# The setup of a two-layer transformer kernel made shorter, its modulated rows moved to GpSimd, and the first batch's reciprocals placed behind the next tile's maxima

## The reference, cut to what matters

```python
mod = (_silu(L0_c) @ L0_wmod).reshape(B, 6, 1, -1)         # [16,256] @ [256,1536], once per layer
sa, ca, ga, sb, cb, gb = (mod[:, i] for i in range(6))
ga = (2 * (ga >= 0) - 1) * max(abs(ga), 0.25)              # gb alike
h = layernorm(x) * (1 + ca) + sa
x = x + ga * local_attention_and_mlp(h)                    # q, k, v, band softmax, Wo, layernorm, gelu MLP
h = layernorm(x) * (1 + cb) + sb
x = x + gb * sorted_experts(h)                             # the first 1024 rows, top 2 of 8 experts
# the second layer: mod from L1_c, L1_wmod; linear attention, grouped-query attention, experts by capacity
```

## Time and profile before

| | us |
|---|---|
| median of 3 runs (lowest, highest) | 3178.84 (3176.0, 3182.64) |
| the profiled execution's own time | 3183.52 |
| its span | 3181.8 |
| setup block, until all engines pass its end | 29.1 |
| tile 0 of batch 0: first row maximum | 45.3 |
| tile 0 of batch 1: first row maximum | 94.7 |

### The profile page before, as it was taken

The page is one execution under the profiler, slowest core; times in us unless marked ns, Lnnn a source line. Parts: engine busy times, 40 slices in busy tenths (PEclk is TensorE's granted clock), DMA queues, the critical chain, the costliest instruction groups (busy, mean ns, idle before and its releaser), DMA issues. The chain is left out here.

```text
span 3181.8 us, 58120 instructions
## 1 busy us (share of the span) xinstructions
PE 3018.6 (95%) x19338; PEld 1850.6 (58%) x19338; DVE 2186.8 (69%) x6717; ACT 1562.6 (49%) x3529; POOL 1213.6 (38%) x1530
## 2 busy tenths in 40 slices
PE   7899999999998998899999999999999968999997
PEld 3566766666665674344444444444444327888886
DVE  6777777777763333678888888888888842445545
ACT  3566556565552113466666666666666631111111
POOL 3123232232234212234444444444443242455544
PEclk8899999999999999899999999999999989999998
DMA  8111010110122981222222222222222217999995
GB/s 292 7 53 45 33 64 33 33 64 33 35 100 79 315 297 52 71 58 68 73 74 74 75 71 73 73 77 78 78 78 73 80 35 213 242 272 280 272 263 173
DMA packets 291041, 354.70 MB, mean 111 GB/s; under 512 B 49855, under 2 KB 240562, under 8 KB 290752
## 3 DMA queue, kind: packets, MB, share of 16 engines
q1 hardware_dynamic: 261760, 313.28, 31.2%
q0 software_dynamic: 28464, 34.71, 5.0%
q10 hardware_dynamic: 544, 3.15, 0.3%
HBM read 234.02 MB, written 122.34 MB: 112 GB/s over the span
## 5 line engine op out<-in xcount | busy, mean ns | idle before, releaser
L2907 DVE TENSOR_REDUCE negmax<-psum 128x1 f32<-128x512 f32 x1024 | 670.7, 685 | 129.7 <-PE psum L3487 125.1
L2520 ACT ACTIVATE pT<-psum 128x512 f32<-128x512 f32 x1024 | 576.8, 600 | 258.8 <-PE psum L3513 225.4
L3487 PE MATMUL psum<-k_stack,q_stack 96*128 96x512 bf16 x1024 | 357.0, 388 | 17.4 <-DVE negmax L2907 10.3
L3513 PE MATMUL psum<-q_stack,k_stack 99*128 99x512 bf16 x1024 | 347.8, 382 | 8.1 <-ACT pT L2520 6.2
L4149 POOL DMA_INDIRECT src_rows<-ye,place x142 | 221.9, 1563 | 283.3 <-DVE ye L4208 251.7
L990 ACT ACTIVATE probs<-probs,negmax 128x256 f32<-128x256 f32 x512 | 252.8, 495 | 119.0 <-DVE negmax L1081 117.4
L4166 ACT ACTIVATE actT_x<-psum 128x512 f32<-128x512 f32 x142 | 84.8, 597 | 441.4 <-PE psum L4323 441.4
L3527 PE MATMUL psum<-pT,v_tile 128*32 128x512 f32 x2048 | 273.3, 606 | 1.6 <-ACT pT L2520 1.0
L4323 PE MATMUL psum<-xT_x,w_x 128*128 128x256 f32 x1136 | 260.3, 383 | 1.1 <-DMA w_x<-in_L_ffn_w_dram 1.1
L4335 PE MATMUL psum<-w_x,actT_x 128*128 128x256 f32 x1136 | 256.6, 379 | 0.0
L1081 DVE CUSTOM_DVE_ANT_0 probs<-psum,band_mask 128x256 f32<-128x256 f32 x512 | 181.6, 421 | 104.8 <-PE psum L1339 104.7
(11 more groups left out here) (420 smaller groups left out, 5602.8 us busy)
## 6 DMA issues: line engine op xcount, KB each, us to landing
w_x<-in_L_ffn_w_dram SPq DMA_DIRECT2D x142, 512.0 KB, 5.4
w_e<-in_L_ffn_w_dram SPq DMA_DIRECT2D x46, 1024.0 KB, 6.4
q_stacks<-q_part SPq DMA_DIRECT2D x192, 128.0 KB
q_stack<-q_stacks SPq DMA_DIRECT2D x64, 384.0 KB, 3.7
padded<-w_e SPq DMA_DIRECT2D x32, 650.0 KB, 6.0
xe<-padded SPq DMA_DIRECT2D x71, 260.0 KB, 5.2
gate_rows<-mods SPq DMA_DIRECT2D x66, 256.0 KB, 5.6
src_e<-src_rows SPq DMA_DIRECT2D x30, 512.0 KB, 6.5
```

Source lines behind the costliest of these rows:

```text
L2520: act.activation(pT[:, 4 * (s % 2) + r, :], bank(m, 2 + n % 2), ACT.Exp, scale=float(DHQ) ** -0.5)\
L2907: dve.tensor_reduce(negmax[:, p // REP, h:h + 1], bank(m, max_bank(b, 16 * g + p)), AX.X, ALU.max, negate=True).then_inc(max_read, 1)
L3487: pe.matmul(bank(m, max_bank(b, 16 * g + p)), q_stack[0:K_SCORE, h, t * P:(t + 1) * P], k_stack[0:K_SCORE, g, :], start=True, stop=True).t ...
L3513: pe.matmul(bank(m, 2 + n % 2), k_stack[:, g, kc * P:(kc + 1) * P], q_stack[:, REP * g + r, :], start=True, stop=True).then_inc(sT_done, 1)
```

## The change

Setup computes layer 0's modulation alone, with the columns that batch 0 needs for its projections (two of six slots). Layer 0's nine rows are made in the next block by GpSimd (`first_rows`), ahead of `hidden_rows(0)`. Layer 1's product with `wmod` and the expert counts go into the next block on TensorE. The loads are put in another order, scratch tiles lie in x's room for batches 7 to 15, and VectorE's reciprocals of tiles 0 to 2 in batch 0 stand behind the next tile's maxima. Cut to its core:

```diff
@@ setup_block, SyncE
             for layer in (0, 1):
                 sp.dma_start(cond[:, layer, :], I[f"L{layer}_c"]).then_inc(cond_in, 16)
-            load_batch(0)
...
-            load_attention_weights(sp, m, I)
-            load_batch(1)
+            load_x(sp, m, I, 0, m.x_first)
+            load_attention_weights(sp, m, I)
+            sp.dma_start(m.wmod1[:, :, :], I["L1_wmod"].rearrange("(c p) n -> p c n", p=P)).then_inc(m.x_second, 16)
+            load_x(sp, m, I, 1, m.x_second)
...
             for i, n in enumerate(("L1_attn_bo", "L1_ffn_ob")):
                 sp.dma_start(m.bias1[:, i, :], I[n].partition_broadcast(B)).then_inc(m.bias1_in, 16)
-            sp.wait_ge(rows_ready, 8)
-            sp.dma_start(mods_dram[0, :, :, :], rows[:, :, :]).then_inc(m.rows_out, 16)
+            load_small_weights(sp, m, I)
@@ setup_block, TensorE
+            pe.wait_ge(wmod_in, 16)
+            for n in range(NBLK):
...
             pe.wait_ge(m.xn0_ready, NT)
...
+            pe.wait_ge(scale_ready, 1)
+            for i in (0, 1):
...
@@ local_attention_block, SyncE
+            load_mlp_weights(sp, m, I)
+            sp.wait_ge(rows0_ready, 8)
+            sp.dma_start(mods_dram[0, :, :, :], m.rows0[:, :, :]).then_inc(m.rows_out, 16)
             sp.wait_ge(m.rows_out, 16)
             load_norm_rows(0)
             load_gate_rows(0)
-            load_mlp_weights(sp, m, I)
@@ local_attention_block, GpSimd
+            def first_rows():
+                mod, sign, rows, bias = m.mod0, m.sign0, m.rows0, m.bias0
+                gates = mod[:, 2:6:3, :]
+                step = Steps(pool, rows0_s, 0, 0)
+                step(pool.tensor_scalar(sign[:, :, :], gates, 0.0, 0.5, ALU.is_ge, ALU.subtract))
+                pool.wait_ge(m.bias1_in, 16 * 7)
+                step(pool.tensor_tensor(bias[:, 0, :], bias[:, 0, :], bias[:, 2, :], ALU.add))
+                step.settle()
+                step(pool.tensor_tensor(gates, gates, sign[:, :, :], ALU.mult))
+                pool.tensor_scalar(rows[:, 7, :], mod[:, 4, :], 1.0, None, ALU.add).then_inc(rows0_ready, 1)
+                step.settle()
+                step(pool.tensor_scalar(gates, gates, 0.125, 4.0, ALU.max, ALU.mult))
+                pool.tensor_copy(rows[:, 8, :], mod[:, 3, :]).then_inc(rows0_ready, 1)
+                step.settle()
+                step(pool.tensor_tensor(rows[:, 0:3:2, :], gates, sign[:, :, :], ALU.mult))
+                pool.tensor_copy(rows[:, 4, :], mod[:, 1, :]).then_inc(rows0_ready, 1)
+                step.settle()
...
+                pool.tensor_tensor(rows[:, 1, :], rows[:, 1, :], sign[:, 0, :], ALU.add).then_inc(rows0_ready, 3)
+
+            first_rows()
             hidden_rows(0, 0)
@@ local_attention_block, VectorE, body, for each of tiles 0 to 2
                 if cur:
                     copy_probsT(b, 0)
-                    invert(b, 0)
+                    if not first:
+                        invert(b, 0)
...
                 if cur:
                     row_max(b, 1)
+                    if first:
+                        invert(b, 0)
                     normalise(b, 0)
@@ local_attention_block, TensorE
+            pe.wait_ge(m.x_second, 32)
+            second_modulation(0)
             pe.wait_ge(hT_act, 1)
...
+            pe.wait_ge(mod1_read, 3)
+            pe.wait_ge(ranks_read, 3)
             body(0, 0, first=True)
```

More of the change, by code:

```diff
@@ L314, in setup_block @@
         cond = sb("cond", [B, 2, D])
[L315 to L333, removed]
+        wmod = sb("wmod", [P, C, 6 * D])
+        expT = sb("expT", [P, 2 * C * B])
         cond_in = sem("cond_in")
-        bias_in = sem("bias_in")
-        wmod_in = [sem("wmod_in0"), sem("wmod_in1")]
+        wmod_in = sem("wmod_in0")
         zeroed = sem("zeroed")
         constants = sem("constants")
+        route_c = sem("route_constants")
         exp_done = sem("exp_done")
@@ L384, in _ @@
[L384 to L391, removed]
@@ L472, in _ @@
-            dve.tensor_copy(rows[:, 8, :], mod[:, 3, :]).then_inc(rows_ready, 1)
-            step.settle()
-            dve.wait_ge(rows_ready, 6)
-            dve.scalar_tensor_tensor(out=rows[:, 1, :], in0=rows[:, 3, :], scalar=later[:, 0:1], in1=rows[:, 1, :],
-                                     op0=ALU.mult, op1=ALU.add).then_inc(rows_ready, 2)
+            dve.wait_ge(mod_read, 1)
+            dve.tensor_scalar(m.mod0[:, 1, :], m.mod0[:, 1, :], 1.0, None, ALU.add).then_inc(scale_ready, 1)
@@ L517, in _ @@
                 mm.then_inc(m.hT_done, 1)
+            pe.wait_ge(scale_ready, 1)
+            for i in (0, 1):
+                for c in range(C):
+                    j = (i * C + c) * B
+                    mm = pe.transpose(bank(m, 6)[:, j:j + B], m.mod0[:, i, c * P:(c + 1) * P], m.ident[0:B, 0:B])
+            mm.then_inc(cols_done, 1)
 def local_weights(nc, m, ctx):
@@ L794, in _ @@
             for b in range(4, B):
+                if b == LATE:
+                    sp.wait_ge(mod1_done, 3)
+                    sp.wait_ge(rank_done, 1)
                 load_x(sp, m, I, b, m.x_rest)
@@ L1239, in body @@
                     copy_probsT(b, 1)
-                    invert(b, 1)
+                    if not first:
+                        invert(b, 1)
                     residual(b, 0, spare(9), par)
@@ L1248, in body @@
                     copy_probsT(b, 2)
-                    invert(b, 2)
+                    if not first:
+                        invert(b, 2)
                     residual(b, 1, spare(16), par)
@@ L1257, in body @@
                     row_max(b, 3)
+                    if first:
+                        invert(b, 2)
                     normalise(b, 2)
                 if first:
-                    dve.wait_ge(m.x_third, 32)
+                    dve.wait_ge(m.x_third, 64)
                     first_norm0(dve, m, b + 2)
```

198 lines of the change are left out of this document (112 added, 86 removed).

## The result

The changed kernel took 3195.77 us (median of 5 runs, 3189.85 to 3200.09) against 3179.46 us (3176.0 to 3183.89) for the kernel before: ratio 1.0043, 95% interval 1.003 to 1.0055, or 9.5 to 17.5 us, with 13.7 for the ratio itself. A second set of runs gave 3198.28 us and 1.0056 (1.0042 to 1.007), or +17.8 us. In one later set two executions of the kernel before, of 9186 and 11778 us, were slow ones and are in no ratio.

A forecast was written before the change was run, and what follows sets the result against it. TensorE, busy 3018.6 of 3181.8 us, was taken as the bound, idle mainly in the first slices. Shifts of 1.0 (start and rows), 7.8 (reciprocals) and 0.7 (clock) gave +9.5 us: 3188.3 for the median, range 3179 to 3197.

The forecast's parts named there:

- Term 1: Setup block: with work moved out, the second block starts at 21.0 in place of 29.12 us, a gain of 8.1.
- Term 2: Rows on GpSimd ahead of batch 0's hidden rows: the gain is lost, shift of +1.0 us at tile 0's copies.
- Term 3: Batch 0, tiles 0 to 2: reciprocals behind the next maxima delay TensorE's transposes by 3.0, 3.6 and 1.2, sum +7.8 us.
- Term 4: TensorE's clock: projections behind the two new waits run partly at the lower clock, +0.7 us, ends 0 and 3.4.
- the ring: Stretch from tile 0's copies to batch 1's first maximum; 41.66 us before, 55.17 after, 53.57 in the repeat.
- The third rival: Slower still: lower clock in both gaps (+3.4), or start at 23 to 25 (+2 to +4); 3192 to 3197 us, chance 0.15.

The follow-up runs named there:

- the repeat: The changed kernel run and traced once more, nothing altered; 3198.28 us, ratio 1.0056 to the kernel before.
- experiment 4: Against the changed kernel with reciprocals at their old place: GpSimd's shift of batch 0's rows held until VectorE wrote batch 1's xn; ratio 1.0003 to the kernel before.
- experiment 2: Against the changed kernel: TensorE transposes the reciprocals behind the projection, ratio 1.0018; or six useless matmuls fill each wait, 1.0035 (both to the kernel before).

## Why the prediction was right in sign and short in size

**Term 1** held: start at 20.0 for a forecast of 21.0, inside its bounds. TensorE's own work ended at 17.3 (16.89 and 0.42), and the start followed `bv_rows`, issued at 14.24 and 3.78 long.

**Term 2** held in its chain: `first_rows` 13.1 (13.3 forecast), from the start to xn 24.5 (24.7). Its last link was mis-sized: xn, taken as 1.37, was 3.09 and 4.21. The first maximum at 47.52 met the forecast of 47.1 by luck: the start was 1.0 better and this link 1.7 worse. At tile 0's copies the shift was +0.4 in the first run and +2.7 in the repeat, for +1.0 with ends 0.2 and 1.8.

The Trainium skill, "SBUF — State Buffer", section "Who interferes with whom", lists `tensor_scalar` among the VectorE operations that can enter a mode which takes the ports shared with GpSimd. The prediction used that section for instructions with two inputs only. The rows of experiment 4 agree with the wider rule: each of the four VectorE instructions, 0.41 us alone, ended 0.14 or 0.15 us behind one of GpSimd's.

**Term 3** held, tile by tile: by the table of experiment 2 the waits cost 2.4, 3.4 and 1.3 us (3.9, of which 2.6 are hidden behind tile 2) for 3.0, 3.6 and 1.2, together 7.0 for 7.8.

**Term 4 is the step that failed in size**: +0.7, ends 0 and 3.4, where the rows behind the two waits show 5.2 in the first trace and 4.2 in the repeat (3.6 to 5.5 in six), and the ring with what stands ahead of the first wait 6.5 and 4.9. The prediction had let most of the slowness "only move from what ran at it before", and its upper end prices about one projection. In fact both projections ran longer, q by 2.5 (1.7 in the repeat) and k by 2.3 or 2.4, behind 3.8 and 3.8 us (2.9 and 3.8) in which TensorE stood idle; with the idle time filled they took 3.60. The third rival ("the lower clock in both gaps") had the mechanism, and +3.4 of its price.

**Not in the prediction**: the stall in batch 14 and the clock behind it, 1.4 us in the first trace and 3.0 in the repeat.

**The sum**: 0.4 + 7.0 + 6.5 = 13.9 at batch 1, as read, and 2.7 + 7.0 + 4.9 = 14.6 in the repeat; 14.8 and 17.0 at batch 15; 13.7 and 17.8 at the end, by the ratios. That a shift behind batch 0 passes through one to one held for the change. For the kernel with the reciprocals back it did not: +8.0 at batch 15, but +2.2 at the end, with an interval from -0.6 to +5.1. Marks are read from one trace, ratios from many runs, and from batch 15's mark to the end single traces of these kernels take 2259.9 to 2273.2 us; where the difference comes from stays open.

## What to carry to other kernels

A reciprocal, or any small step, that another engine consumes ahead of its long work must not be queued behind a block of instructions that itself waits for that engine: the three waits here cost 7 us, and the lower clock behind them 4 to 5 more. Work moved off a long block is a gain only if the first consumer behind it doesn't read the result: two of nine rows were on the path, and making these first brought batch 1 forward by 2.9 us; in time it ended level. When code gets shorter or longer, look once more at the "issue" gaps far behind it.

## What the runs showed of the hardware

- Four VectorE `tensor_scalar` of 128x256 from SBUF to SBUF took 1.37 to 1.38 us alone and 3.09 or 4.21 beside GpSimd's `tensor_tensor`, which itself lost 0.12. Each ended 0.14 to 0.16 us behind the end of a GpSimd instruction; in the longer form the last one ended behind a GpSimd memset of 1.18 us.
- VectorE stood still once in batch 14 for nothing that the profile shows, at a place that moved with the length of the code ahead. This cost 1.0 to 1.2 us with no traffic beside it, 2.3 beside 0.4 MB, 3.9 to 4.3 beside the zero stores. The Trainium skill, "Runtime: NRT & Kernel Launch", section "Instruction fetch mechanics", has code come in blocks of 16 KiB and calls the cost of crossing a boundary mostly hidden. The transfer that goes with this stall has 8 KB. Over the whole program the traces agree with "mostly hidden": VectorE shows one such gap of over 0.9 us in the kernel before and two in the repeat. The one in batch 14 was not hidden.
- Six matmuls in a wait of 3.8 us, which left 1.0 us of it idle, brought the projection behind it from 6.09 back to 3.60. The Trainium skill, "TensorE: Matmul & The Clock Gate", Part 1, has idle stretches fall back to the lower state; the rows agree (granted clock 0.55 from 60 to 65 us, and 1.00 with the filler).
